# Softmax of the cloud layers on each query's own third of the scores, and one packed input transfer at the head

## The reference, cut to what matters

```python
x = x + _L0_xattn_ref(_layernorm(x, axis=-1), ctx_4096, x1_scale, x1_zp, x2_scale, x2_zp)
x = x + _L0_attn_ref(_layernorm(x, axis=-1), ...)
x = x + _L0_ffn_ref(_layernorm(x, axis=-1), ...)
x = x + _L1_xattn_ref(ctx_4096, _layernorm(x, axis=-1), ...)
x = x + _L1_attn_ref(...)
x = x + _L1_ffn_ref(...)
```

```python
def fake_quant(x, scale, zp):
    q = jnp.clip(jnp.round(x / s + z), QMIN, QMAX)
    return (q - z) * s
return jnp.matmul(fake_quant(x1, ...), fake_quant(x2, ...))
```

```python
gf = jnp.concatenate([jnp.broadcast_to(center, (B, N, k, C)), neigh - center], axis=-1)
...
qh = x16.reshape(B * N, k, nheads, headdim)
scores = jnp.einsum('bihd,bjhd->bhij', qh, qh) / np.float32(np.sqrt(headdim))
attn = jax.nn.softmax(scores, axis=-1)
out = jnp.einsum('bhij,bjhd->bihd', attn, qh).reshape(B * N, k, total)
fused = out @ W_lin.T + b_lin
```

## Time and profile before

| | us |
|---|---|
| median of 3 runs | 1002.33 |
| lowest, highest | 1000.74, 1005.09 |
| the profiled execution | 1002.12 |
| its span | 1000.5 |

### The profile page before, as it was taken

The page is one execution under the profiler, slowest core; times in us unless marked ns, Lnnn a source line. Parts: engine busy times, 40 slices in busy tenths (PEclk is TensorE's granted clock), DMA queues, the critical chain, the costliest instruction groups (busy, mean ns, idle before and its releaser), DMA issues. The chain is left out here.

```text
span 1000.5 us, 38062 instructions
## 1 busy us (share of the span) xinstructions
PE 958.8 (96%) x15968; PEld 734.6 (73%) x15968; DVE 735.7 (74%) x1932; ACT 467.5 (47%) x765; POOL 449.5 (45%) x408
## 2 busy tenths in 40 slices
PE   3899999999999999999989999999999999999998
PEld 1699878696969687765977777768866666665695
DVE  6698747956657483797968888978788888887410
ACT  6343324141423323212377777774576767674010
POOL 1101211630212202020299999960798888886000
PEclk9999999999999999999999999999999999999999
DMA  8997797877887796566213222231222222221660
GB/s 339 406 407 280 257 326 268 332 285 279 309 301 295 255 350 232 184 259 254 92 39 73 66 71 65 70 78 66 68 68 64 53 62 55 60 56 41 252 253 22
DMA packets 58794, 182.42 MB, mean 182 GB/s; under 512 B 9193, under 2 KB 10969, under 8 KB 58330
## 3 DMA queue, kind: packets, MB, share of 16 engines
q1 hardware_dynamic: 55058, 172.03, 49.2%
q0 software_dynamic: 2432, 8.42, 2.4%
q10 hardware_dynamic: 1224, 0.81, 0.4%
HBM read 154.45 MB, written 1.61 MB: 156 GB/s over the span
## 5 line engine op out<-in xcount | busy, mean ns | idle before, releaser
L558 PEld LDWEIGHTS ps<-hT,ring 128*128 128x128 f32 x2304 | 258.3, 192 | 6.7 <-issue 6.5
L558 PE MATMUL ps<-hT,ring 128*128 128x128 f32 x2304 | 260.1, 276 | 0.0
L2040 POOL TENSOR_TENSOR X<-sortedT,ring 128x960 f16 (+1 forms) x84 | 158.8, 1891 | 21.0 <-PE ps L1614 20.9
L991 POOL TENSOR_TENSOR y_y<-y_z,sgate 128x512 f32<-128x512 f32 x16 | 20.1, 1273 | 192.6 <-DVE y_z L922 192.6
L2065 POOL TENSOR_TENSOR PP<-S,PP 128x480 f16<-128x480 f32 x86 | 100.0, 1163 | 5.3 <-ACT PP L1808 5.3
L1633 PE MATMUL ps<-PT,ring 128*64 128x120 f16 x2752 | 97.4, 222 | 5.0 <-DMA PT<-P_turned 2.3
L591 PE MATMUL ps<-wt,y_n 128*128 128x512 f32 x224 | 99.4, 596 | 1.5 <-DVE xs L914 1.5
L1633 PEld LDWEIGHTS ps<-PT,ring 128*64 128x64 f16 x2752 | 84.3, 110 | 18.4 <-issue 8.0
L1808 ACT CAST PP<-S 128x480 f16<-128x480 f32 x86 | 67.0, 779 | 60.5 <-POOL S L2058 60.5
L2058 POOL TENSOR_TENSOR S<-S,den 128x480 f32<-128x480 f32 x86 | 88.9, 1033 | 3.7 <-DVE den L1935 3.7
L821 DVE SCALAR_TENSOR_TENSOR xc<-xpad,parg,xc 128x128 f32<-128x128 f32 x192 | 59.2, 371 | 42.3 <-ACT xc L705 41.1
(11 more groups left out here) (330 smaller groups left out, 1555.9 us busy)
## 6 DMA issues: line engine op xcount, KB each, us to landing
ring<-in_w_in SPq DMA_DIRECT2D x36, 2048.0 KB, 9.4
wt<-in_w_out SPq DMA_DIRECT2D x14, 2048.0 KB, 7.7
PT<-P_turned SPq DMA_DIRECT2D x332, 64.0 KB, 2.0
ring<-in_w SPq DMA_DIRECT2D x8, 1024.0 KB, 12.1
ctx_chunks<-in_ctx SPq DMA_DIRECT2D x4, 1024.0 KB, 10.9
krow<-keys_scratch POOLq DMA_DIRECT2D x8, 512.0 KB, 7.0
mchunk<-in_mask_t POOLq DMA_DIRECT2D x8, 512.0 KB, 8.1
ring<-in_w_out SPq DMA_DIRECT2D x2, 2048.0 KB, 8.2
```

The costliest lines, as they stand in the source:

```text
L558: mm = nc.tensor.matmul(ps[:, bank, j * T:(j + 1) * T], weights[:, j, kc * P:(kc + 1) * P], k.hT[:, kc, :], start=kc == 0, stop=kc == KC - 1)
L2040: ins = gp.tensor_tensor(fcopy(c.X[u][:, 0, 0:1], full(cnt)), fcopy(c.fsT[:, 0, bass.ds(it * STEP, 1)], trio(start, cnt, 1)), fcopy(c.fTr[ ...
```

## The change

It has two parts. **At the head** the four scalars, the two per-head parameters and the turned coordinates are laid side by side into one input `head_in` of 128 x 54 floats, which SP loads right behind x. The four scalar transfers, the two coordinate transfers, the one of `head_par`, PE's turning and ACT's copy of the coordinates go. The addition of the row term to x moves from DVE to ACT, behind ACT's last chunk; DVE waits for it there.

**In the cloud layers** the mask product goes. PE writes the 30 columns of a slot into three separate thirds of the bank. A constant `own_third` (128 x 3, 0 or 1) tells which third belongs to a partition's row. DVE picks: third 0 times its flag, plus third 1 times its flag, plus third 2 times its flag, giving `E` of 128 x 160. Maximum, subtraction, exp and sum work on these 160 elements. `den_own` (128 x 48) is the reciprocal times the three flags, and POOL's normalisation multiplies `E`, repeated three times, by `den_own`, which writes all 480 elements of `S` with zeros outside the own third. PE does the transposes ahead of the scores. POOL's differences wait for the scores of two steps before in place of the transposes, the pick waits for POOL's normalisation of two steps before, and the normalisation waits for POOL's own lower half of two steps before. POOL builds one small constant in place of two masks.

The diff, cut to its core:

```diff
@@ first stage
-        sc = k.sb("scales", [P, 4], F32, ctx)
+        sc = k.head_in[:, 0:4]
...
             sp.dma_start(k.x[:, :], dr["x"]).then_inc(s_x, 16)
+            sp.dma_start(k.head_in[:, :], dr["head_in"]).then_inc(s_sc, 16)
             for c in range(CHUNKS):
                 load_chunk(c)
-            sp.dma_start(k.head_par[:, :], dr["head_par"]).then_inc(k.head_par_in, 16)
...
-            v.wait_ge(s_sc, 64)
+            v.wait_ge(s_sc, 16)
...
-            v.wait_ge(s_row, 5)
-            nc.vector.tensor_scalar(k.x[:, :], k.x[:, :], rowb[:, 3:4], None, ALU.add).then_inc(s_q1, 1)
-            v.wait_ge(s_q1, 4)
+            v.wait_ge(s_row, 6)
...
-            for i, name in enumerate(("L0_xattn_x1_scale", "L0_xattn_x1_zp", "L0_xattn_x2_scale", "L0_xattn_x2_zp")):
-                act.dma_start(sc[:, i:i + 1], dr[name].partition_broadcast(P)).then_inc(s_sc, 16)
...
+            act.wait_ge(s_row, 5)
+            nc.scalar.activation(k.x[:, :], k.x[:, :], ACT.Identity, bias=rowb[:, 3:4], scale=1.0).then_inc(s_row, 1)
@@ cloud layers, PE
-                for r in range(2):
-                    half = slice(r * C, (r + 1) * C)
-                    nc.tensor.matmul(ps[:, S_BANK + r, 0:COLS], c.rows_u[half, :], c.cols_v[half, :, :].rearrange("p s i -> p (s i)"),
-                                     start=True, stop=False)
...
-                            mm = nc.tensor.matmul(ps[32 * q:32 * q + 32, S_BANK + r, slot * ROWS:(slot + 1) * ROWS], X[half, ab, at:at + 32],
-                                                  X[half, ab, at:at + ROWS], start=False, stop=slot == SLOTS - 1)
+                            thirds = ps[32 * q:32 * q + 32, S_BANK + r, 0:COLS].rearrange("p (w s j) -> p w s j", w=TRIO, j=WIN)
+                            mm = nc.tensor.matmul(thirds[:, :, slot, :], X[half, ab, at:at + 32],
+                                                  X[half, ab, at:at + ROWS], start=True, stop=True)
...
+                rows(*lagged(0))
                 scores(*lagged(0))
-                rows(*lagged(0))
@@ cloud layers, DVE
-                scores = ps[:, S_BANK:S_BANK + 2, 0:COLS].rearrange("p r (s i) -> p r s i", i=ROWS)
-                vec.tensor_reduce(c.mx[u][:, :].rearrange("p (r s) -> p r s", r=2), scores, AX, ALU.max).then_inc(s_max, 1)
+                third = lambda w: ps[:, S_BANK:S_BANK + 2, w * SLOTS * WIN:(w + 1) * SLOTS * WIN]
+                vec.tensor_scalar(E, third(0), own[:, 0:1], None, ALU.mult).then_inc(s_sel, 1)
+                v.wait_ge(s_sel, 2 * t0 + it * 2 + 1)
+                vec.scalar_tensor_tensor(out=E, in0=third(1), scalar=own[:, 1:2], in1=E, op0=ALU.mult, op1=ALU.add).then_inc(s_sel, 1)
+                v.wait_ge(s_sel, 2 * t0 + it * 2 + 2)
+                vec.scalar_tensor_tensor(out=E, in0=third(2), scalar=own[:, 2:3], in1=E, op0=ALU.mult, op1=ALU.add).then_inc(s_read, 1)
+                v.wait_ge(s_read, t0 + it + 1)
+                vec.tensor_reduce(c.mx[u][:, :], c.E[u][:, :, :], AX, ALU.max).then_inc(s_max, 1)
                 v.wait_ge(s_max, t0 + it + 1)
-                vec.tensor_tensor(S[:, :, :].rearrange("p (r s) i -> p r s i", r=2), scores,
-                                  fcopy(c.mx[u][:, :], [[SLOTS, 2], [1, SLOTS], [0, ROWS]]), ALU.subtract).then_inc(s_sub, 1)
+                vec.tensor_tensor(c.E[u][:, :, :], c.E[u][:, :, :], fcopy(c.mx[u][:, :], [[1, 2 * SLOTS], [0, WIN]]), ALU.subtract).then_inc(s_sub, 1)
...
-                vec.tensor_reduce(c.den[u][:, :], c.S[u][:, :, :], AX, ALU.add).then_inc(s_den, 1)
-                v.wait_ge(s_den, 2 * t0 + it * 2 + 1)
+                vec.tensor_reduce(c.den[u][:, :], c.E[u][:, :, :], AX, ALU.add).then_inc(s_den, 1)
+                v.wait_ge(s_den, 3 * t0 + it * 3 + 1)
                 vec.reciprocal(c.den[u][:, :], c.den[u][:, :]).then_inc(s_den, 1)
+                v.wait_ge(s_den, 3 * t0 + it * 3 + 2)
+                vec.tensor_tensor(c.den_own[u][:, :, :], fcopy(c.den[u][:, :], [[1, 2 * SLOTS], [0, TRIO]]),
+                                  fcopy(c.own[:, :], [[0, 2 * SLOTS], [1, TRIO]]), ALU.mult).then_inc(s_den, 1)
@@ cloud layers, POOL
+            eng.tensor_tensor(c.S[u][:, :, :].rearrange("p s (w j) -> p s w j", j=WIN), fcopy(c.E[u][:, 0, :], [[WIN, 2 * SLOTS], [0, TRIO], [1, WIN]]),
+                              fcopy(c.den_own[u][:, 0, :], [[TRIO, 2 * SLOTS], [1, TRIO], [0, WIN]]), ALU.mult).then_inc(s_P, 1)
...
-                    pool.wait_ge(s_xt, t0 + it - 1)
+                    pool.wait_ge(s_S, t0 + it - 1)
...
-                gp.tensor_tensor(S, S, fcopy(c.den[ph % 2][:, :], [[1, 2 * SLOTS], [0, ROWS]]), ALU.mult).then_inc(s_P, 1)
```

More of the change, by code:

```diff
@@ L1315, in __init__ @@
         self.PP = [k.sb(f"PP{u}", [P, 2 * SLOTS, 32, 2], F16) for u in range(2)]
[L1316 removed]
+        self.own = k.sb("own_third", [P, TRIO], F32)
         self.conv_d, self.blocks = k.sb("conv3_diagonal", [P, 2, P], F32), k.sb("blocks", [P, P], F32)
@@ L1329, in cloud_constants @@
         gp.memset(whole[(slice(None),) * len(whole.shape)], 0.0).then_inc(c.filled, 1)
-    gp.memset(c.rows_u[:, :], 1.0).then_inc(c.filled, 1)
-    gp.memset(c.cols_v[:, :, :], -FAR).then_inc(c.filled, 1)
+    gp.memset(c.own[:, :], 1.0).then_inc(c.filled, 1)
     gp.iota(c.iota[:, :], [[1, N]], base=0, channel_multiplier=0, allow_small_or_imprecise_dtypes=True).then_inc(c.filled, 1)
-    pool.wait_ge(c.filled, 12)
+    pool.wait_ge(c.filled, 11)
     for q in range(4):
         gp.memset(c.blocks[32 * q:32 * q + 32, 32 * q:32 * q + 32], 1.0).then_inc(c.filled, 1)
-    pool.wait_ge(c.filled, 16)
-    made = 0
-    for r in range(2):
-        half = slice(r * C, (r + 1) * C)
[L1340 to L1346, removed]
-            gp.affine_select(out=m, in_=m, compare_op=ALU.is_ge, fill=value, base=30, pattern=[[0, cnt], [0, m.shape[2]]],
-                             channel_multiplier=-1).then_inc(c.shaped, 1)
-            pool.wait_ge(c.shaped, made + 3)
-            gp.affine_select(out=m, in_=m, compare_op=ALU.is_ge, fill=0.0, base=31, pattern=[[0, cnt], [0, m.shape[2]]],
-                             channel_multiplier=-1).then_inc(c.shaped, 1)
-            made += 4
-    pool.wait_ge(c.shaped, made)
+    pool.wait_ge(c.filled, 15)
+    for q in range(4):
+        rows = c.own[32 * q:32 * q + 32, :]
+        gp.affine_select(out=rows, in_=rows, compare_op=ALU.is_ge, fill=0.0, base=0, pattern=[[-WIN, TRIO]], channel_multiplier=1).then_inc(c.shaped, 1)
+    pool.wait_ge(c.shaped, 4)
+    for q in range(4):
+        rows = c.own[32 * q:32 * q + 32, :]
+        gp.affine_select(out=rows, in_=rows, compare_op=ALU.is_ge, fill=0.0, base=WIN - 1, pattern=[[WIN, TRIO]], channel_multiplier=-1).then_inc(c.shaped, 1)
+    pool.wait_ge(c.shaped, 8)
 def weight_products(nc, pe, k, layer):
@@ L1387, in __init__ @@
         self.den = [sb(f"den{u}", [P, 2 * SLOTS]) for u in range(2)]
+        self.E = [sb(f"E{u}", [P, 2 * SLOTS, WIN]) for u in range(2)]
+        self.den_own = [sb(f"den_own{u}", [P, 2 * SLOTS, TRIO]) for u in range(2)]
         self.PT = k.PT
@@ L1585, in scores @@
                     return
-                pe.wait_ge(s_X, t0 + it + 1)
-                if after(it, 1):
-                    pe.wait_ge(s_sub, t0 + it)
                 X = c.X[ph % 2]
-                for r in range(2):
-                    half = slice(r * C, (r + 1) * C)
-                    nc.tensor.matmul(ps[:, S_BANK + r, 0:COLS], c.rows_u[half, :], c.cols_v[half, :, :].rearrange("p s i -> p (s i)"),
-                                     start=True, stop=False)
                 for slot in range(SLOTS):
@@ L1607, in rows @@
                     return
+                pe.wait_ge(s_X, t0 + it + 1)
+                if after(it, 1):
+                    pe.wait_ge(s_read, t0 + it)
                 if after(it, 2):
```

49 lines of the change are left out of this document (20 added, 29 removed).

## The result

The changed kernel takes 1039.68 us in the median of 4 runs (1038.69 to 1041.03) against 1002.22 for the kernel before (4 runs). The ratio is 1.037, with a 95% interval of 1.035 to 1.039: slower by 37.5 us, where 1041 was forecast. The span of the profiled execution is 1037.9 us.

The account below looks back on a forecast made before the run. POOL was taken to bound layer 1 and PE layer 2, with DVE close behind. Terms 30 + 3.5 + 2.5 + 4 + 1.2 - 1.7 = +39.5, added to 1002.1, gave 1041 us; likeliest case 1028 to 1060.

Parts of the forecast that it names:

- Head: Kernel start: one packed transfer replaces four small ones DVE idles 2.00 us for; -1.7 us, bounds 1.0 and 2.2.
- DVE's own work: DVE in each cloud step: picks and shorter operations replace the 480-element reduce and subtraction; net +0.45 us per step.
- The port: Cloud steps: a DVE instruction with two SBUF inputs waits for the running POOL instruction; subtraction asked at 2.2, done 3.06.
- The step: One cloud step, counted from den_own's end to the next, with the port wait: 4.6 us in both layers.
- Layer 1: Cloud layer 1: step grows from 3.87 to 4.6 us over 41 steady steps; +30 us.
- Layer 2: Cloud layer 2: +3.5 us for the first five steps, +2.5 for 36 steps, +4 for missed boundaries.
- steps that miss their boundary: Layer 2: one step in eight waits for POOL's third instruction as well, about +0.9 us each; +4 us.
- Filling and draining: Ends of each cloud layer: transposes ahead of the scores on PE and one longer DVE chain; +1.2 us.
- POOL keeps the port while it has work: Rival, cloud steps: the subtraction waits for POOL's whole burst; 5.6 us a step, about 1120 us; chance 0.25.
- The partial waits: Rival, cloud steps: the subtraction's request settles near the boundary, costing 0.2 to 0.4 a step; 1008 to 1025 us; chance 0.07.
- The lower clock: Rival: something slower still, such as a lower TensorE clock once PE idles in layer 1; no size; chance 0.05.
- the loop doesn't meet the port: Rival, cloud loop: no port wait; layer 1 stays 3.87, layer 2 gains 4; about 997.5 us; chance 0.13.

Follow-up runs that it names:

- no_port: The changed kernel with the maximum in spare PSUM columns and, from step 6 of each layer, the denominators in PSUM too; 1008.94 us (ratio 1.0066).
- mx_in_psum: The changed kernel with the maximum written to spare PSUM columns, so the subtraction has one SBUF input; 1012.33 us (ratio 1.011).
- act_pick: The changed kernel with the maximum in PSUM, den_own made by three multiplications by one flag each, and the first pick moved to ScalarE; 1017.71 us (ratio 1.016).
- no_port_pick: As no_port, and from step 8 on ScalarE does the first of the three picks; 996.00 us (ratio 0.9936 to the kernel before).

## Why the prediction was right, and where it was off

- **Head, -1.7.** 3.2 was measured at the first cloud step, and 2.0 to 2.6 in the run with the head alone. The mechanism held and was larger than the 2.0 put down as the most it could gain: DVE's parameters start at 7.53, where they started at 11.18, and of the 3.7 us 1.6 come from x itself, which lands at 4.52 in place of about 6.1. The sum had taken x's landing as fixed. That the six small transfers issued by ACT had delayed it is the likely reason; none was tried alone.
- **DVE's own work, +0.45 a step.** Mean durations of the pick 0.375, the multiply-adds 0.384 each, the reduce 0.320 and the free subtraction 0.32: the prices from neighbouring sizes (0.36, 0.38, 0.31, 0.32) hold within 0.02.
- **The port.** The subtraction was forecast asked for at 2.2 and done at 3.06 after den_own's end in layer 1. It was asked for 2.16 and done 3.10 after it (601.38, 603.54, 604.48). The Trainium skill ("SBUF — State Buffer", Who interferes with whom) calls the pair of ports that the two engines share an exclusive lock, for which a DVE instruction with two SBUF inputs contends with a GpSimd instruction that reads SBUF. These runs agree: 0.28 for the one input and 1.13 for the two, with X running.
- **The step, 4.6.** By the starts of POOL's normalisation it is 4.46 in three of four steps of layer 1 and 4.55 in the fourth. The terms add up to 4.59, 0.13 too long. The 0.1 for the semaphore ahead of POOL stood in the sum twice, at its head and at its end. The transpose starts 0.07 before the subtraction's record ends (604.41 and 604.48), which the sum left out, and the subtraction is done 0.04 later than taken. From start to start the rest held: 0.63, 0.31 and 0.28 for 0.62, 0.31 and 0.29.
- **Layer 1, +30.** +26.7. Layer 2, +10 with the steps that miss their boundary: +12.4. There the mechanism was right, and the count and the price of the misses were wrong. Not one step in eight missed it by chance but exactly one in four, where DVE's loop turns: DVE's next statistics come 0.46 later, and the subtraction is asked for behind X's end and inside L2055, so the step grows from 4.46 to 5.61:

```profile
794.72 0.73 DVE L1876 BATCH_NORM_STATS2 stats<-ps 128x240 f32 x2 [0.46 <-issue]
...
797.14 1.12 POOL L2055 TENSOR_TENSOR PP<-S,PP 128x480 f16<-128x480 f32 x1
...
797.53 0.92 DVE L1902 TENSOR_TENSOR E<-E,mx 128x160 f32<-128x160 f32 x1
...
799.96 1.02 POOL L1478 TENSOR_TENSOR S<-E,den_own 128x480 f32<-128x480 f32 x1 [1.69 <-DVE den_own L1925]
```

  The other three of four wait little, 0.05 to 0.15 us, and take 4.46 to 4.54. No_port, where no pair is left by then, has 4.43 to 4.52 there, so these steps are set by DVE's own chain and not, as the forecast had it, by the port's boundary. A step with a miss is 1.1 to 1.2 longer than its neighbours, where 0.9 was taken; about 0.5 of it is the loop's turn itself, which no_port shows too (4.94 for 4.43).
- **Filling and draining, +1.2.** The stretch between the layers shows +2.3 and the end -0.8: about as forecast. The 2.3 isn't the subtraction's wait, since mx_in_psum and no_port show 51.6 and 52.3 there as well; which part of the drain holds it is open.
- **The rivals.** That POOL keeps the port while it has work would have given 5.6 a step (its terms add up to 5.68); it was 4.46. The partial waits of 0.2 to 0.4 a step would have ended at 1025 at most. The lower clock, put in for something slower still, did come, but only in the filling of each layer (below). That the loop doesn't meet the port would have given 997.5; no_port, without such pairs but for its first six steps, came to 1008.9. So that rival was priced too low: the sum gave DVE 4.4 in layer 2, which three of four steps show, and left out the 0.4 to 0.5 us of the fourth, and what the filling costs (the first six steps of layer 1 take 24.2 us in no_port and 22.6 before). In no_port den_own's waits of those six steps stand in the filling, and PE waits for the subtraction, not for the third pick; both may hold a part of it.
- **The total.** The terms of the forecast add up to 1041.6, and 1039.7 was measured. The nearness owes something to terms that missed on both sides: layer 1 was 3.3 too high and the head gained 1.5 more than taken, while layer 2 was 2.4 too low.

## What to carry to other kernels

Before an instruction is moved or cut down on DVE, count its SBUF inputs and look at what POOL does at that moment: in layer 1 a subtraction over 160 elements with two SBUF inputs took 0.95 us, and one over 480 read from PSUM took 0.66. Where an operand is small, a few spare columns of a PSUM bank that DVE owns at that time take the wait away, here 0.6 us a step of layer 1, of which the step got 0.4 back. Cutting POOL's instruction into pieces brought nothing here, in one run: it moved the boundary at which DVE is let in, the next pair waited instead, and POOL's pieces together took longer.

## What the runs showed of the hardware that was not expected

- Small multiplications by a per-partition flag, 128x16 in SBUF with one tensor input, took 0.23 each, started 0.14 apart, and waited for POOL as the pairs do (0.86 beside L2062 in act_pick). One tensor input in SBUF is therefore not enough to stay clear of POOL; the reductions, with one input as well, never waited. The Trainium skill ("SBUF — State Buffer", Who interferes with whom) counts `tensor_scalar`, which these are, among the operations that can enter a mode with two ports and then contend with GpSimd, and says of `tensor_reduce` on this chip that it never contends: the two measured cases agree, though no run here shows which of the ports was held.
- TensorE's clock fell to 1.2 GHz in the filling of both layers of the changed kernel, and stays at 1.00 in the kernel before's. In the stretch ahead of the fall in layer 1 PE had been busy for 1.62 of 4 us (508 to 512), where the kernel before has 3.13. Two stretches at the lower level, in layer 1, and one of no_port_pick:

```profile
512.00:516.00 4.00, 2.59 (x81) 2.21 (x81) 3.83 (x9) 2.58 (x5) 3.55 (x4) 0.50 0.24 56
...
522.00:524.00 2.00, 2.00 (x11) 0.82 (x9) 1.98 (x3) 0.81 (x2) 2.00 (x2) 0.50 0.18 43
```

```profile
512.00:516.00 4.00, 3.18 (x104) 2.77 (x104) 3.78 (x10) 3.02 (x7) 3.86 (x4) 0.63 0.22 52
```

  By the subtractions the step from 521.49 to 527.58 took 6.09 us, but the next only 4.20. By POOL's normalisations the longest step of that filling is 5.12 (524.59 to 529.71) where its neighbours take 4.46, so the lower clock can have cost about 0.7 us in layer 1, and by the same reckoning 0.2 in layer 2. That the port's wait made the clock fall isn't shown: it fell in no_port_pick too (0.63) and in layer 2 of no_port (0.70 from 740 to 744), where no subtraction waits.
- The turn of a loop costs DVE 0.4 to 0.5 us of idle time, once in four steps. In the kernel before it was hidden in both layers, under POOL's and PE's step; with DVE's chain as the bound it shows in full.
